# Narrow heads of a twelve-layer decoder: first loads from two queues, head weights compacted by pieces, moves issued by two engines, rows of maxima awaited by group

## What is computed

```python
x = _layernorm(x + _L0_attn_ref(x, ...))   # part 0: 16 heads of width 16, with biases, causal
...
x = _layernorm(x + _L2_attn_ref(x, ...))   # part 6: 2 x 16 heads of width 8, causal
# part 0
scores = jnp.where(causal, einsum(q, k) * SCALE, -jnp.inf)
ctx = einsum(softmax(scores), v);  return ctx @ w_proj.T + b_proj
# part 6: two softmaxes for each head, one taken from the other
lam = exp(dot(lambda_q1, lambda_k1)) - exp(dot(lambda_q2, lambda_k2)) + LAMBDA_INIT
diff = A1 - lam * A2;  diff = (1 - LAMBDA_INIT) * diff / rms(diff);  return diff @ Wproj
```

## Time and profile before

| what | us |
|---|---|
| median of the three runs (lowest, highest) | 2368.63 (2368.13, 2379.76) |
| the profiled execution, its own time | 2365.69 |
| its span, first to last instruction | 2364.1 |
| busy in the span: PE, DVE, ACT, POOL | 1892.7, 1375.7, 894.0, 314.5 |
| L0a: PE's first projection, first score, first transposed score | 23.98, 46.83, 82.67 |
| L2a: the same three | 769.42, 804.18, 872.50 |

### The profile page before, as it was taken

The page is one execution under the profiler, slowest core; times in us unless marked ns, Lnnn a source line. Parts: engine busy times, 40 slices in busy tenths (PEclk is TensorE's granted clock), DMA queues, the critical chain, the costliest instruction groups (busy, mean ns, idle before and its releaser), DMA issues.

```text
span 2364.1 us, 29032 instructions
## 1 busy us (share of the span) xinstructions
PE 1892.7 (80%) x10398; PEld 1305.4 (55%) x10398; DVE 1375.7 (58%) x2535; ACT 894.0 (38%) x2121; POOL 314.5 (13%) x265
## 2 busy tenths in 40 slices
PE   5664768747735777689998979979999999999895
PEld 3432444414412445566666748865666766667652
DVE  3359956869988461666666128883666235554214
ACT  1335512145422116366665036433555034443000
POOL 2303520005500105111111000000000000000100
PEclk9985568765557889899999999997999999999876
DMA  4010020010010210000001010000001000000000
GB/s 115 8 37 0 1 60 0 5 56 0 1 45 1 39 48 2 14 14 16 13 13 56 8 73 1 1 1 7 9 11 49 1 18 12 13 30 1 36 1 18
DMA packets 25742, 49.18 MB, mean 21 GB/s; under 512 B 6262, under 2 KB 19603, under 8 KB 24092
## 3 DMA queue, kind: packets, MB, share of 16 engines
q1 hardware_dynamic: 25644, 47.85, 6.7%
HBM read 42.20 MB, written 1.05 MB: 18 GB/s over the span
## 4 chain that ended last, share of the span: by engine, by line
PE 57%; DVE 27%; issue 7%; ACT 5%; SPq 2%; DMA 1%; POOL 1%; DVEq 0%; ACTq 0%; POOLq 0%; PEldq 0%
PE banks L1322 7%; PE banks L1249 7%; PE banks L1312 7%; DVE big L936 6%; PE banks L1283 6%; PE banks L1304 3%; DVE big L556 3%; PE banks L1564 2%; PE banks L1974 2%; PE banks L1953 2%; PE banks L463 2%; PE banks L474 2%; ACT big L2080 2%; DVE big L1658 1%; PE banks L1270 1%
## 5 line engine op out<-in xcount | busy, mean ns | idle before, releaser
L1399 DVE COPY arena<-banks 128x512 f32<-128x512 f32 x196 | 135.3, 690 | 259.2 <-PE banks L1304 255.4
L1312 PE MATMUL banks<-arena,big 128*128 128x256 f32 x784 | 217.5, 400 | 9.0 <-DVE arena L1399 8.9
L1283 PE MATMUL banks<-big 128*128 128x256 f32 x784 | 209.6, 391 | 1.6 <-ACT big L1436 1.6
L222 POOL TENSOR_TENSOR ln_rstd<-ln_var_eps,neg_half 128x2 f32<-128x2 f32 x48 | 37.8, 787 | 1249.8 <-DVE ln_var_eps L210 1249.8
L1462 ACT ACTIVATE arena<-banks,arena 128x256 f32<-128x256 f32 x392 | 193.3, 501 | 19.0 <-DVE arena L1354 15.7
L1249 PE MATMUL banks<-x_feat,arena 128*128 128x512 f32 x392 | 178.2, 598 | 1.2 <-ACT big L1446 1.2
L1480 ACT ACTIVATE big<-banks 128x256 f32 (+1 forms) x196 | 75.3, 384 | 274.6 <-PE banks L1312 274.6
L1312 PEld LDWEIGHTS banks<-arena,big 128*128 128x128 f32 x784 | 139.6, 191 | 66.6 <-DVE arena L1399 52.5
L1322 PE MATMUL banks<-arena,big 128*128 128x256 f32 x784 | 174.3, 382 | 1.9 <-ACT big L1480 1.9
L1322 PEld LDWEIGHTS banks<-arena,big 128*128 128x128 f32 x784 | 147.5, 190 | 27.5 <-issue 4.6
L1354 DVE TENSOR_REDUCE arena<-banks 128x2 f32<-128x512 f32 x196 | 134.4, 686 | 41.2 <-PE banks L1283 41.1
(11 more groups left out here) (309 smaller groups left out, 3333.2 us busy)
## 6 DMA issues: line engine op xcount, KB each, us to landing
big<-big SPq DMA_DIRECT2D x32, 64.0 KB, 2.3
arena<-in_L0f_w SPq DMA_DIRECT2D x1, 2048.0 KB, 8.3
arena<-in_L1a_wo SPq DMA_DIRECT2D x1, 2048.0 KB
arena<-in_L1f_gv SPq DMA_DIRECT2D x1, 2048.0 KB
arena<-in_L2a_qk_w SPq DMA_DIRECT2D x1, 2048.0 KB
big<-big SPq DMA_DIRECT2D x64, 32.0 KB
arena<-in_L2x_wo SPq DMA_DIRECT2D x1, 2048.0 KB
arena<-in_L2x_q_w SPq DMA_DIRECT2D x16, 128.0 KB, 2.0
```

The costliest lines, as they stand in the source:

```text
L1283: last = mm(ps[:, h * SEQ:(h + 1) * SEQ], q[:, b * SEQ + h * P:b * SEQ + (h + 1) * P], k[:, b * SEQ:(b + 1) * SEQ], start=not self.mask, s ...
L1312: last = mm(slot, self.v[:, 2 * b + kc, :], self.probs_t[:, u % 2, kc, :], start=(kc == 0), stop=(kc == 1))
L1399: v.tensor_copy(self.probs_t[:, u % 2].rearrange("p a b -> p (a b)"), B[4 + u % 2][:]).then_inc(self.turn_read, 1)
```

## The change

- First loads. x_feat has a semaphore of its own (feat_loaded). In L0a ACT issues the q and k weights and the sixteen bias rows, SyncE the rest, with x_tok and ctx_feat (x_loaded, now 32) behind v's weights. DVE's program still begins with a wait for x_loaded.
- Weights. The eight copies signal prepared once for each block and side, and PE waits for the piece that it multiplies next. The bias is scaled after them (b_scaled, which ACT waits for), the product for lambda comes after them too, and its exponential moves behind ACT's moves.
- Ones. DVE fills k with 1.0; the four DMAs of ones are gone. In L0a this fill stands ahead of the copies. A move waits for all three fills (cleared is 3: q, v and k).
- Moves. ACT issues the moves of q of a block right behind that block's staging, SyncE those of k.
- Rows of maxima. rows_moved is two semaphores, by parity of the group. A transposed score waits for its own group's rows at the group's first unit, not for all rows at the start; the first score_t stands ahead of the last turn_max and waits for the reduction that frees its slot.
- sum_up does the block below the diagonal first, and waits for the mask only ahead of the diagonal blocks.

```diff
@@ -169,10 +169,10 @@
 
 
     def wait_x_tok(self, eng, l):
-        eng.wait_ge(*((self.x_ready, TILES * l) if l else (self.x_loaded, 48)))
+        eng.wait_ge(*((self.x_ready, TILES * l) if l else (self.x_loaded, 32)))
 
     def wait_x_feat(self, eng, l):
-        eng.wait_ge(*((self.xt_ready, 4 * l) if l else (self.x_loaded, 48)))
+        eng.wait_ge(*((self.xt_ready, 4 * l) if l else (self.feat_loaded, 16)))
 
 
 
...
@@ -318,44 +318,43 @@
         e, l, d, n, w = self.e, self.l, self.e.dram, self.name, self.width
         if l >= 2:
             sp.wait_ge(e.xt_ready, 4 * (l - 1))
-        loads = [(self.qk_w, d[n + "_qk_w"].rearrange("g p s c f -> p g s c f")), (self.v_w, d[n + "_v_w"]), (self.proj_w, d[n + "_proj_w"])]
-        if not self.diff:
-            loads += [(self.v_b, d[n + "_v_b"].rearrange("a b -> (a b)").partition_broadcast(P)),
-                      (self.proj_b, d[n + "_proj_b"].rearrange("a b -> (a b)").partition_broadcast(P))]
-            for g in range(self.groups):
-                blk, at = divmod(g, self.per_block)
-                for j in range(4):
-                    row = (4 * at + j) * w
-                    loads += [(self.qk_b[row:row + w, blk, :], d[n + "_qk_b"][32 * j:32 * j + w, g, :])]
+            sp.dma_start(self.qk_w, d[n + "_qk_w"].rearrange("g p s c f -> p g s c f")).then_inc(self.qk_loaded, 16)
+        sp.dma_start(self.v_w, d[n + "_v_w"]).then_inc(self.w_loaded, 16)
+        if self.diff:
+            sp.dma_start(self.lam_in, d[n + "_lam"].partition_broadcast(P)).then_inc(self.w_loaded, 16)
         else:
-            loads += [(self.lam_in, d[n + "_lam"].partition_broadcast(P))]
-        for dst, src in loads:
-            sp.dma_start(dst, src).then_inc(self.w_loaded, 16)
-        if self.hosts:
-            self.beside.load(sp)
-        e.wait_x_feat(sp, l)
-        sp.wait_ge(e.consts_made, 1)
-        sp.wait_ge(self.k_cleared, 1)
-        for j in range(4):
-            row = 32 * j + w
-            sp.dma_start(self.k[row:row + 1].rearrange("o g t -> o (g t)"), e.ones[0:TILES * self.groups, :]).then_inc(self.moved[0], 16)
+            sp.dma_start(self.v_b, d[n + "_v_b"].rearrange("a b -> (a b)").partition_broadcast(P)).then_inc(self.w_loaded, 16)
+            sp.dma_start(e.x_tok[:], d["x"].rearrange("b (h p) d -> p (b h) d", p=P)).then_inc(e.x_loaded, 16)
+            sp.dma_start(e.ctx_feat[:], d["ctx_feat"]).then_inc(e.x_loaded, 16)
+            sp.dma_start(self.proj_b, d[n + "_proj_b"].rearrange("a b -> (a b)").partition_broadcast(P)).then_inc(self.w_loaded, 16)
+        sp.dma_start(self.proj_w, d[n + "_proj_w"]).then_inc(self.w_loaded, 16)
         for blk in range(2):
-            for s in range(2):
-                sp.wait_ge(self.staged, 4 * blk + 2 * s + 2)
-                sp.wait_ge(self.cleared, 1)
-                for at in range(self.per_block):
-                    for j in range(4):
-                        row = (4 * at + j) * w
-                        dst = (self.k if s else self.q)[32 * j:32 * j + w, blk * self.per_block + at, :]
-                        sp.dma_start(dst, self.stage[row:row + w, s, blk, :]).then_inc(self.moved[blk], 16)
+            self.move(sp, blk, 1)
         for g in range(self.groups):
             sp.wait_ge(self.max_read, g + 1)
+            if g >= 2:
+                sp.wait_ge(self.rows_moved[g % 2], 64 * (g // 2))
             for j in range(4):
                 row = 32 * j + w
-                sp.dma_start(self.q[row:row + 1, g, :], self.max_rows[8 * j:8 * j + 8, g, :]).then_inc(self.rows_moved, 16)
+                sp.dma_start(self.q[row:row + 1, g, :], self.max_rows[8 * j:8 * j + 8, g, :]).then_inc(self.rows_moved[g % 2], 16)
+
+    def move(self, queue, blk, s):
+
+        w = self.width
+        queue.wait_ge(self.staged, 4 * blk + 2 * s + 2)
+        queue.wait_ge(self.cleared, 3)
+        for at in range(self.per_block):
+            for j in range(4):
+                row = (4 * at + j) * w
+                dst = (self.k if s else self.q)[32 * j:32 * j + w, blk * self.per_block + at, :]
+                queue.dma_start(dst, self.stage[row:row + w, s, blk, :]).then_inc(self.moved[blk], 16)
 
     def host(self, beside):
         self.beside = beside
+
+    @property
+    def n_loads(self):
+        return 3 if self.diff else 4
 
     def room(self):
 
...
@@ -386,12 +385,11 @@
         e, nc, l = self.e, self.e.nc, self.l
         B, G, mm = e.bank, self.groups, self.e.nc.tensor.matmul
         e.wait_x_feat(pe, l)
-        pe.wait_ge(self.prepared, 1)
-
         if self.hosts:
             self.beside.tensor_in(pe)
         for blk in range(2):
             for s in range(2):
+                pe.wait_ge(self.prepared, 2 * blk + s + 1)
                 for half in range(2):
                     bank = B[self.proj_bank(blk, s, half)]
                     if blk and self.hosts:
...
@@ -442,16 +441,18 @@
                 turn_max(u // 4 - 1)
             for n in self.first_slots(u):
                 self.beside.tensor_slot(pe, n)
-        turn_max(G - 1)
+        if self.hosts:
+            turn_max(G - 1)
 
         def score_t(u):
             g, b = divmod(u, 4)
             slot, masked = self.slot(u), not self.hosts
-            if u == 0:
-                pe.wait_ge(self.rows_moved, 16 * 4 * G)
-                if self.hosts:
-                    pe.wait_ge(self.max_read, G)
-            if u >= self.slots:
+            if b == 0:
+                pe.wait_ge(self.rows_moved[g % 2], 64 * (g // 2 + 1))
+            if u < self.slots:
+                pe.wait_ge(self.maxed, self.units - self.slots + u + 1)
+                pe.wait_ge(self.max_read, G - self.slots + 1 + u)
+            else:
                 pe.wait_ge(self.exped, 2 * (u - self.slots) + 2)
                 pe.wait_ge(self.sum_read, u - self.slots + 1)
             for j in range(0 if masked else 4):
...
@@ -467,8 +468,10 @@
         def sum_up(u):
             g, b = divmod(u, 4)
             slot = self.slot(u)
-            pe.wait_ge(self.exped if self.hosts else self.masked, 2 * u + 2)
-            for half, kc, first in ((0, 0, True), (1, 0, True), (1, 1, False)):
+            pe.wait_ge(self.exped, 2 * u + 2)
+            for half, kc, first in ((1, 0, True), (0, 0, True), (1, 1, False)):
+                if half == kc and not self.hosts:
+                    pe.wait_ge(self.masked, 2 * u + 2)
                 for j in range(4):
                     at = kc * SEQ + (half - kc) * P
                     last = mm(B[slot + half][32 * j:32 * j + 32, 3 * P:4 * P], self.v[:, 2 * b + kc, 4 * (g % 4) + j, :],
...
@@ -518,24 +522,29 @@
     def vector(self, dve):
         e, nc, G = self.e, self.e.nc, self.groups
         B, ch = e.bank, e.dve_chain
-        dve.wait_ge(self.w_loaded, self.n_loads)
+        if self.l == 0:
+            nc.vector.memset(self.k, 1.0).then_inc(self.cleared, 1)
+        dve.wait_ge(self.qk_loaded, 16)
+        for blk in range(2):
+            for s in range(2):
+                heads = self.qk_w[:, blk * self.per_block:(blk + 1) * self.per_block, s].rearrange("p g c (j f) -> p c g j f", f=32)
+                for c in range(CH):
+                    ins = nc.vector.tensor_copy(self.compact_w[:, blk, s, c, :].rearrange("p (g j f) -> p g j f", g=self.per_block, j=4), heads[:, c, :, :, 0:self.width])
+                    ins.then_inc(self.prepared, 1) if c else ch.mark(ins)
+        ch.join(dve)
+        if self.l:
+            e.wait_x_feat(dve, self.l)
+            nc.vector.memset(self.k, 1.0).then_inc(self.cleared, 1)
+        if not self.diff:
+            dve.wait_ge(self.b_loaded, 64 * G)
+            nc.vector.tensor_scalar(self.qk_b[:, :, 0], self.qk_b[:, :, 0], self.scale, None, ALU.mult).then_inc(self.b_scaled, 1)
+        dve.wait_ge(self.w_loaded, 16 * self.n_loads)
         if self.diff:
             ch.link(dve, nc.vector.tensor_tensor(self.lam_prod, self.lam_in[:, 0:4:2, :], self.lam_in[:, 1:4:2, :], ALU.mult))
             nc.vector.tensor_reduce(self.lam_dot, self.lam_prod, AX.X, ALU.add).then_inc(self.lam_dots, 1)
-        else:
-            ch.mark(nc.vector.tensor_scalar(self.qk_b[:, :, 0], self.qk_b[:, :, 0], self.scale, None, ALU.mult))
-        for blk in range(2):
-            for s in range(2):
-                for c in range(CH):
-                    heads = self.qk_w[:, blk * self.per_block:(blk + 1) * self.per_block, s, c, :].rearrange("p g (j f) -> p g j f", f=32)
-                    ch.mark(nc.vector.tensor_copy(self.compact_w[:, blk, s, c, :].rearrange("p (g j f) -> p g j f", g=self.per_block, j=4), heads[:, :, :, 0:self.width]))
-        ch.join(dve)
-        dve.sem_inc(self.prepared, 1)
-        e.wait_x_feat(dve, self.l)
-        nc.vector.memset(self.k, 0.0).then_inc(self.k_cleared, 1)
         if self.hosts:
             self.beside.vector_conv(dve)
-        dve.wait_ge(self.cleared, 2)
+        dve.wait_ge(self.cleared, 3)
         for pair in range(4):
```

(23 more changed lines are left out.)

19 lines of the change are left out of this document (10 added, 9 removed).

## The result

The changed kernel takes 2358.24 us in the median of 6 runs (2356.21 to 2364.09), the kernel before in the same comparison 2371.0 us (2365.61 to 2379.76): a ratio of 0.9944, 95% interval 0.9919 to 0.9969. It is faster by 0.3 to 0.8%, 12.8 us between the medians, where 26.0 were forecast; its time lies 1.2 us above the range.

What follows compares the result with a forecast made beforehand. The chain was taken to run through PE and DVE, with little in SyncE's queue and DMA. Terms 2.0 + 10.2 + 2.0 - 2.5 + 11.1 + 1.2 + 2.0 = 26.0 us, off the 2368.63 median: 2342.6 us, range 2334 to 2357.

Steps and rivals of the forecast that it cites:

- Change of phase, 5.55 us twice: L0a and L2a: exponential follows the last read of maxima without four moves, landing and score between, 5.55 us each.
- Without the gap the clock should stay, 2.0 us, or 0: L2a, exponential to fourth score: 8.16 us at low clock, 6.14 in L0a; full clock would gain 2.0 us, or 0.
- Moves of L2a, 10.2 us: L2a before the first score: no moves of ones, two queues issuing 16 each; 10.2 us gained, bounds 11.0 and 8.6.
- rival 3: The two queues take turns, so 32 moves take 21.4 us as now; 2366.9 us, chance 0.11.
- 2.0 - 2.5: L2a's first scores: 2.0 us gained by full clock, 2.5 lost as ACT's second moves delay its read of maxima.
- Front of L0a, 2.0 us: Start of L0a: earlier loads and piecewise waits start PE at 22.0 us instead of 23.98, gaining 2.0 us.
- less 0.39 MB at 0.4 MB/us that is about 13.4: Front of L0a: estimate of when x_tok and ctx_feat have landed, ending DVE's first wait, taken as 13.6 us.
- the lower bound: Front of L0a: the clear of k holds POOL up, PE starts at 22.9 us, gain only 1 us.
- ScalarE's moves in L0a cost nothing: L0a, PE's start to the maxima: ACT's eight moves before staging block 1 are covered, 18.1 us against 22.6 needed; 0.
- Order of sum_up, 1.2 us: Both stages: first third of sum_up no longer awaits the mask, about 0.3 us at first and last unit, 1.2 total.
- Rival 2: An ACT DMA costs 1.0 us, not 0.67; 15.7 us gained in all, 2352.9 us, chance 0.12.
- rival 5: The early transposed score does not keep the clock: 2 us less, 2344.6 us; chance 0.52 jointly with the forecast.

Runs made afterwards that it cites:

- fill: The changed kernel plus matmuls whose results nobody reads, placed where TensorE waits in L0a and L2a: 2349.97 us, ratio 0.9888 to the kernel before.
- after: The changed kernel itself, in its first profile: 2358.24 us in the median, 2360.71 us in the profiled execution.
- after2: The changed kernel run and profiled once more, nothing edited: 2357.86 us, ratio 0.9922 to the kernel before.
- front_old: The changed kernel with the front of L0a (loads, clear of k, copies, projections) as before the change: 2359.33 us, ratio 0.9929.
- best1: The changed kernel with VectorE's first wait and clear of k later, L2a's lambda exponential before staging, ScalarE issuing only first-block q moves: 2345.72 us.
- front_free: The changed kernel with VectorE's first wait moved to the first norm and L0a's clear of k behind copies and scaling: 2345.98 us, ratio 0.9877.
- wait_free: The changed kernel with only VectorE's first wait moved to the first norm, clear of k staying first: 2349.45 us, ratio 0.9876.
- k_late: The changed kernel with only L0a's clear of k put behind the eight copies and the scaling: 2351.10 us, ratio 0.9899.

## Why the prediction was right and wrong

The terms of the sum, and what stands for each in the first pair of profiles (us gained, less is a loss):

| stretch | forecast | measured |
|---|---|---|
| L0a, to the first score | +2.0 | -1.5 |
| L0a, first score to last read of maxima | 0 | 0 |
| L2a, to the first row of scores | +10.2 | +9.3 |
| L2a, from there to the last read of maxima | +2.0 - 2.5 | +1.1 - 4.4 |
| last read to first exponential, both stages | +11.1 | +11.3 |
| first exponential to last transposed score, L0a | none | -1.4 |
| the same, L2a | +2.0 | -4.6 |
| last transposed score to the stage's end, L0a, L2a | none | +1.8, -2.5 |
| order of sum_up, both stages | +1.2 | in the three rows above |
| the ten other stages | none | -4.0 |
| sum | +26.0 | +5.0 |

- **Change of phase, 5.55 us twice: right as a mechanism.** Read to exponential shrank by 5.66 in L0a and 5.67 in L2a.
- **"Without the gap the clock should stay, 2.0 us, or 0", of L2a: wrong, and the largest miss.** From the exponential to the last transposed score L2a took 79.5 us after and 74.8 before: 4.6 lost where 2.0 were to be won. The gap of 4.15 us went, but gaps of 0.3 to 0.75 us remained one after another, and the clock fell to 0.50 all the same, 2 us behind the exponential, for 20.5 us instead of 13.7. The step took a low clock in one profile as the price of one long gap. fill shows that with all these gaps filled it stays. In L0a after, after2 and front_old show that its length is a matter of the execution; in L2a what sets it stays open.
- **Moves of L2a, 10.2 us: right.** Measured 9.3 at the first row of scores (9.7 at the first product), inside 8.6 to 11.0. ScalarE's moves cost 0.80 us and SyncE's 0.73, not 0.67, which put the first score at 25.5 us against 24.6. The Trainium skill ("Perfetto Trace Analysis", section "DMA Instruction — HWDGE (DVE, Sync)") has two sequencers exclude each other while descriptors are made; whether they did no row shows. If so, it cost a fifth of a move at most, and rival 3 at its worst, where each move takes twice as long, is out.
- **"2.0 - 2.5" for the first scores of L2a: mis-sized.** From the first row of scores to the first turn of maxima it took 9.5 us and not 8.6 (10.6 before): 1.1 gained, since the clock fell for 3.4 us at 798. From that turn to the last read 4.4 us were lost, not 2.5: the first read came 2.5 us late, as foreseen (808.60 against a wanted 806.1), but behind it the clock fell again, for 6.8 us. In all, from the first product to the last read, before took 63.3 us and after 67.0; best1, where ScalarE is free in time and the clock stays, takes 61.6.
- **Front of L0a, 2.0 us: wrong in sign for the pair, nothing in the medians.** The step "less 0.39 MB at 0.4 MB/us that is about 13.4", rounded to 13.6 for the end of VectorE's first wait, failed: it ended at 17.37 us, 13.4 us after the issue of ctx_feat, the load it waits for, had begun. That issue alone took 3.17 us while ScalarE's small bias rows were being issued, and in the windows of 9 to 11 us the DMA engines moved 243 and 183 GB/s, not 400. GpSimd began its addition at 17.51, near the 17.0 foreseen. So the lower bound came true in kind, the clear of k held GpSimd up, but with a clear that began 3.8 us late it cost 3.5 us against the forecast and not 1.0. The Trainium skill ("SBUF — State Buffer", section "SBUF: two separate sides") says that GpSimd and a VectorE instruction in a two-port mode exclude each other for the whole of the one that started first. The trace agrees for an addition begun under the clear (7.75 us for 4.49), and for copies (4.51 us for 0.21) and a TENSOR_SCALAR of 128x2 (4.47 us for 0.16) begun under the addition; it does not for the clear itself, which GpSimd's work never held up (front_free, L2a).
- **ScalarE's moves in L0a cost nothing: right**; first score to last read of maxima is 31.20 us before and after.
- **Order of sum_up, 1.2 us: not tested by itself.** TensorE's idle time ahead of the sums fell from 5.1 to 3.0 us over both stages (lines L474 and L477); the stretches around them moved by more than that with the clock.
- **The base.** The sum was made against one profiled execution and taken off a median of three, 2368.63; over 25 runs the median of before is 2374. The profiled execution was a fast one, with 4.0 us less in stages that the change leaves alone. So the difference of the profiles, 5 us, understates the gain, which is 12.8 us in the medians.

Of the rivals none came as told. Rival 2 has the right direction (0.80, not 1.0 us for ScalarE), rival 5 the right place (the clock), but it was thought to be worth 2 us and was worth over 6.

## What to carry to other kernels

A clear or any other independent instruction at the head of an engine's program inherits the waits ahead of it and blocks what follows it: put the wait where its data is used. Where TensorE's work comes in short bursts with half-microsecond gaps, a gain ahead of them can be returned at 1.2 GHz; price it from several executions, and try matmuls nobody reads in the gaps before judging the edit itself. An engine that gets DMAs to issue should get only those that are needed first: in best1 that brought the last read of maxima 5.5 us forward, though the median did not show it while the clock fell behind it. And a row of a merged view can hold a wait: narrow the window before dividing its time by its count.

## What the runs showed of the hardware

- VectorE's copies and TENSOR_SCALAR wait for a GpSimd instruction that is running, a MEMSET included, until its end: eight copies took 7.1 to 7.4 us, one of them 3.6, while GpSimd cleared q and v (front_free, wait_free), and 1.16 us with GpSimd idle or done (k_late, front_old). A GpSimd addition that began 0.14 us into a MEMSET of VectorE took 7.75 us instead of 4.5 (after, after2). But a MEMSET of VectorE that began beside a running addition (3.47 us, front_free) or MEMSET (6.88 us, after) took no longer, nor did they.
- Two queues issuing at once: 0.80 us (ScalarE, its first 1.44) and 0.73 us (SyncE) per 32 KB move instead of 0.67, landing 3.7 us instead of 2.3.
- Behind the change of phase of L0a the same instructions ran 0, 7 or 17 us at 1.2 GHz with the early start (after2, after, front_old), and 7 or 31 before the change.
